# A graph-layer kernel: nineteen whole middle tiles on SyncE's queue in place of fourteen whole and five shared, and no register copy before a row's DMA

## The chip, the cores and the metric

The kernel runs on 1 core of one Trainium2 chip. The metric is the device time of one execution in microseconds. The kernel before takes 1070.66 us, the median of 3 runs (1067.93 to 1071.32). A difference under about 0.3% is no difference that a measurement of this kernel tells.

## What is computed

One relational graph layer with a residual and a normalisation. There are 6250 nodes of 128 features, 106250 edges sorted by destination, and 40 edge types. Cut to what matters:

```
seg = dst * 40 + edge_type
S   = segment_sum(x[src], seg)            # per node and type, 128 features
cnt = segment_sum(1, seg)
agg = einsum('nrd,rdf->nf', S, relation_weights) + cnt @ rFeatures
h   = agg * deg ** -0.5
h   = relu(h + h @ loop_weight)
out = layernorm(x + h)
```

The large irregular part is `x[src]`: 106250 rows of x, fetched by an index that is known only from the input.

## The kernel before

**Tiles and blocks.** The edges are cut into tiles of 128, the nodes into 49 blocks of 128. A block has 17 tiles (`TPB`), 831 tiles are used, and the last of them (tile 830) has 10 edges. For each tile the kernel fetches 128 rows, builds a one-hot matrix of edge types and node positions on VectorE (L815), and multiplies on TensorE (L1027), two matmuls a tile, one for each part of a row: a row of 1 KB in the DRAM tensor `x_parts` holds the features in a high and a low part. ScalarE and VectorE move the result from a PSUM bank into `ring` (L614, L917). Between these, TensorE multiplies the ring by the 40 relation weights and one more matrix (L1039), 82 matmuls (41 pairs) a block. The first 5 blocks fetch plain rows of x instead and split them on the fly, while the same split rows are written to `x_parts` in 13 stages.

**Who fetches the rows.** From block 5 on GpSimd (POOL) fetches a tile with one indirect DMA (L524), in the order of the tiles, into the 17 buffers of `rows`. Before tile t it waits until TensorE is through with tile t - 17 (L523). SyncE (SP) fetches some tiles by itself, row by row: `BY_ROW` lists them, each the middle tile (tile 8 of the 17) of its block, and the last tile. SP's rows go into 8 buffers of their own, which lie in `x_out`, the buffer of the staging; it can begin when the staging is over. For each tile, SP waits until the tile that had its buffer before is done (L471), and then loads up to 16 byte offsets from SBUF into registers (L475), and issues 16 DMAs of one row of 1 KB each, each with a copy of its register (L476, L477). VectorE has made the offsets (L940).

**The shared tiles.** Five of SP's tiles are shared: POOL fetches the first rows of the middle tile in blocks 9, 18, 27, 36 and 45 (126, 124, 127, 112 and 64 of the 128) with one indirect DMA, L509, and SP the rest. SP thus fetches 14 whole tiles (blocks 7, 10, 13 and so on to 46), 87 rows of the shared ones and 10 of the last tile, which is 1889 rows. POOL makes 726 gathers of whole tiles from `x_parts` (L524), 5 of the shared ones, and 85 of plain rows (L531).

**Who waits for the rows.** TensorE waits in `tile` (L1018, L1020) until all rows of the tile have landed. It goes through tiles in order, so a late tile holds all that come after. VectorE waits before its add of tile t (L916) until POOL has issued the gather of tile t + 5.

Of the kernel before, what the change touches and what calls it, by code (L numbers as in the profile page):

```python
# [7 lines left out]
F32 = mybir.dt.float32  # L8
# [3 lines left out]
U8 = mybir.dt.uint8  # L12
F32R = mybir.dt.float32r

P = 128
N, E, D, R = 6250, 106250, 128, 40
# [4 lines left out]
BLOCKS = -(-N // BLOCK)  # L21
LAST_ROWS = N - (BLOCKS - 1) * BLOCK
TPB = 17
# [14 lines left out]
ROW_LOAD = 16  # L38
# [29 lines left out]
FREE_W = 25  # L68
PLAIN_BLOCKS = 5
PLAIN = PLAIN_BLOCKS * TPB  # L70
POOL_PART = {9: 126, 18: 124, 27: 127, 36: 112, 45: 64}
BY_ROW = [i * TPB + TPB // 2 for i in sorted([*range(7, BLOCKS - 1, 3), *POOL_PART])] + [-(-E // P) - 1]
BY_BOTH = {i * TPB + TPB // 2: n for i, n in POOL_PART.items()}
BY_ROW_BUFS = 8
ROW_BYTES = 2 * D * 4
X_ROWS = N // P
# [43 lines left out]
def build(nc, x, src_main, src_by_tile, src_rest, dst_main, dst_rest, type_main, type_rest, r_features, relation_w, loop_w, out):  # L120
    with ExitStack() as ctx:
# [8 lines left out]
        def sem(name):  # L130
            return ctx.enter_context(nc.semaphore(name))
# [141 lines left out]
        by_row_cleared = sem("by_row_cleared")  # L273
        by_row_src_loaded = sem("by_row_src_loaded")
        by_row_ready = sem("by_row_ready")
        both_landed = {t: sem(f"both_landed{t}") for t in BY_BOTH}
        by_row_landed = [sem(f"by_row_landed{j}") for j in range(len(BY_ROW))]
        gathered = [sem(f"gathered{k}") for k in range(TPB)]
        types_ready = sem("types_ready")
# [50 lines left out]
        def rows_in_tile(t):  # L330

            return min(P, E - t * P)

        def first_by_row(t):

            return BY_BOTH.get(t, 0)

        def gathers_through(t):

            return t + 1 - len([n for n in BY_ROW if n <= t and n not in BY_BOTH])  # L340

        def group_of(t):

# [71 lines left out]
        @block.sync  # L415
        def _(sp):
            sp.dma_start(src[:, 0:TPB], src_main[:, 0:TPB]).then_inc(first_src_loaded, 16)
            for t, main in ((dst, dst_main), (typ, type_main)):
                sp.dma_start(t[:, 0:FULL], main).then_inc(edges_loaded, 16)
            sp.wait_ge(padded, 1)  # L420
            for t, rest in ((dst, dst_rest), (typ, type_rest)):
                sp.dma_start(t[0:REST, FULL:FULL + 1], rest).then_inc(edges_loaded, 16)
            sp.dma_start(src[:, TPB:FULL], src_main[:, TPB:FULL]).then_inc(src_loaded, 16)
            sp.dma_start(src[0:REST, FULL:FULL + 1], src_rest).then_inc(src_loaded, 16)

            def stage_load(n):

                p, rows_each, of, _ = stage_rows(n)
                to = x_in[0:p, n % 2, 0:rows_each]
                sp.dma_start(to if rows_each > 1 else to.rearrange("p n d -> p (n d)"), of).then_inc(stage_loaded[n % 2], 16)  # L430

            def stage_store(n):

                p, rows_each, _, to = stage_rows(n)
                of = x_out[0:p, n % 2, 0:rows_each].bitcast(F32)
                sp.wait_ge(stage_low, n + 1)
                sp.dma_start(to, of.rearrange("p n c d -> p n (c d)") if rows_each > 1 else of.rearrange(
                    "p n c d -> p (n c d)")).then_inc(staged[n % 2], 16)

            for n in range(STAGED_FIRST):  # L440
                stage_load(n)
            sp.dma_start(loop[:], loop_w).then_inc(loop_loaded, 16)
            sp.dma_start(x_blk[:], x[0:P, :]).then_inc(x_blk_loaded, 16)
            sp.wait_ge(const_done, 1)
            sp.dma_start(w[0:R, R, :], r_features).then_inc(w_loaded, 16)
            sp.wait_ge(by_row_cleared, 1)
            for j, t in enumerate(BY_ROW):
                of = src_by_tile[t:t + 1, :] if t < FULL else src_rest.rearrange("p o -> o p")
                sp.dma_start(by_row_src[j:j + 1, 0:rows_in_tile(t)], of).then_inc(by_row_src_loaded, 16)
            sp.wait_ge(pos_done, 1)  # L450
            sp.dma_start(pos[:].rearrange("o (b k) -> o b k", k=POS)[:, :, 0:TPB], pos_2d[:, 0:TPB]).then_inc(pos_ready, 16)
            w_v = relation_w.rearrange("r d f -> d r f")
            for r in range(FREE_W, R, W_LOAD):
                sp.dma_start(w[:, r:r + W_LOAD, :], w_v[:, r:r + W_LOAD]).then_inc(w_loaded, 16)
            sp.wait_ge(pos_ready, 16)
            for r in range(0, FREE_W, W_LOAD):
                sp.dma_start(w[:, r:r + W_LOAD, :], w_v[:, r:r + W_LOAD]).then_inc(w_loaded, 16)
            sp.wait_ge(src_loaded, 2 * 16)

            def in_order():  # L460
                for n in range(STAGES):
                    stage_store(n)
                    if n + 2 < STAGES:
                        stage_load(n + 2)
                for h in range(2):
                    sp.wait_ge(staged[h], len(range(h, STAGES, 2)) * 16)
                index = [sp.alloc_register(f"sp_row{n}") for n in range(ROW_LOAD)]
                sp.wait_ge(by_row_ready, 1)
                for j, t in enumerate(BY_ROW):
                    if j >= BY_ROW_BUFS:  # L470
                        sp.wait_ge(tile_done, BY_ROW[j - BY_ROW_BUFS] + 1)  # L471
                    for n, p in enumerate(range(first_by_row(t), rows_in_tile(t))):
                        if n % ROW_LOAD == 0:
                            m = min(ROW_LOAD, rows_in_tile(t) - p)
                            sp.load(index[0:m], by_row_at[j:j + 1, p:p + m])  # L475
                        at = sp.snap(index[n % ROW_LOAD])  # L476
                        sp.dma_start(by_row[p:p + 1, j % BY_ROW_BUFS].rearrange("p c d -> p (c d)").bitcast(U8),  # L477
                                     x_bytes[:, bass.ds(at, ROW_BYTES)]).then_inc(by_row_landed[j], 16)

            def g_load(t):  # L480
                if not isinstance(t, int):
                    sp.wait_ge(g_step, t * G_STEPS + G_SETUP)
                sp.dma_start(g_src[:], src[:, column(t)]).then_inc(g_idx, 16)

            path(sp, in_order, lambda: g_tiles(g_load)(sp))

        @block.gpsimd
        def _(pool):
# [13 lines left out]


            def gather(t):
                if t in BY_BOTH:
                    j, n = BY_ROW.index(t), BY_BOTH[t]
                    if j >= BY_ROW_BUFS:
                        pool.wait_ge(tile_done, BY_ROW[j - BY_ROW_BUFS] + 1)
                    pool.indirect_dma_start(  # L509
                        by_row[0:n, j % BY_ROW_BUFS].rearrange("p c d -> p (c d)").bitcast(F32), None, x_parts,  # L510
                        bass.IndirectOffsetOnAxis(ap=src[0:n, t:t + 1], axis=0), engine_sem=gather_issued).then_inc(
                            both_landed[t], 16)
                    return
                if t in BY_ROW:
                    return
                k = t % TPB
                at_least(pool, gathered[k], gathers_into(k, t - 1) * 16)
                n = rows_in_tile(t)
                if t >= PLAIN:
                    if t == PLAIN:  # L520
                        for h in range(2):
                            pool.wait_ge(staged[h], len(range(h, STAGES, 2)) * 16)
                    pool.wait_ge(tile_done, t - TPB + 1)  # L523
                    pool.indirect_dma_start(  # L524
                        rows[0:n, k].rearrange("p c d -> p (c d)").bitcast(F32), None, x_parts,
                        bass.IndirectOffsetOnAxis(ap=src[0:n, t:t + 1], axis=0), engine_sem=gather_issued).then_inc(
                            gathered[k], 16)
                    return
                if t >= RAW:
                    pool.wait_ge(low_done, group_of(t - RAW) + 1)  # L530
                pool.indirect_dma_start(  # L531
                    raw[:, t % RAW], None, x, bass.IndirectOffsetOnAxis(ap=src[:, t:t + 1], axis=0),
                    engine_sem=gather_issued).then_inc(gathered[k], 16)
# [455 lines left out]
        def _(pe):  # L989
# [12 lines left out]
            def tile(i, k):  # L1002
# [12 lines left out]
                                         hot_node[:, n % TPB], start=True, stop=True)  # L1015
                if not known_less(i, PLAIN_BLOCKS) or not isinstance(i, int):
                    if t in BY_ROW:
                        pe.wait_ge(by_row_landed[BY_ROW.index(t)], (rows_in_tile(t) - first_by_row(t)) * 16)  # L1018
                        if t in BY_BOTH:
                            pe.wait_ge(both_landed[t], 16)  # L1020
                    else:
                        pe.wait_ge(gathered[k], gathers_into(k, t) * 16)
                elif k % 2 == 0:
                    pe.wait_ge(low_done, i * GROUPS + k // 2 + 1)
# [160 lines left out]
```

## Time and profile before

| | |
|---|---|
| median of 3 runs | 1070.66 us |
| the profiled execution | 1068.4 us, its span 1066.5 us |
| TensorE matmul | 954.6 us busy, 90% of the span |
| POOL | 789.6 us busy, 74% |
| VectorE | 742.8 us busy, 70% |
| ScalarE | 532.0 us busy, 50% |
| DMA | 118 GB/s; queue 0 (POOL) 33.5% of the 16 engines, queue 1 (SP) 4.6% |
| mean granted clock of TensorE | 0.985 |

Register moves and the issue of DMAs are not counted as busy, so that SP has no row in this table; its queue (SPq) is read from the timeline and from the rows of its lines. POOL has idle time that is not free: it is the gap from one gather to the next.

### The profile page before, as it was taken

To read this page: it belongs to the slowest core of one execution; us is meant where nothing else is said; L and a number is where in the kernel's file an instruction comes from. 1 tells how busy PE (TensorE), PEld (TensorE's weight loads), DVE (VectorE), ACT (ScalarE), POOL (GpSimd) and SP (SyncE) were. 2 spreads that over 40 slices of the span, in tenths; PEclk is the share of its full clock that TensorE was granted. 3 is DMA by queue.
4 is the path that set the end of the run, shared out by engine and by line. 5 is a ranking of instruction groups with operands and counts; after the bars stand their busy time and mean duration, and the time that the engine had idled before them with its cause. 6 is when DMAs were issued, how large, how long until landed. Compare 5 with 4: busy or idle time off the path is not lost.

```text
span 1066.5 us, 31214 instructions
## 1 busy us (share of the span) xinstructions
PE 954.6 (90%) x6713; PEld 856.4 (80%) x6713; DVE 742.8 (70%) x2590; ACT 532.0 (50%) x1137; POOL 789.6 (74%) x831
## 2 busy tenths in 40 slices
PE   2589999899998989999998899999999899999997
PEld 1369898788888888888887798888888788888887
DVE  6698777676766776667677577767676676767663
ACT  1577555445454545555454355445545554444551
POOL 7777777777777777777777777777777777777770
PEclk9799999999999999999999899999999999999999
DMA  5852234434344443444434344343443344343330
GB/s 166 291 194 56 82 111 116 118 113 115 115 117 113 116 118 112 113 115 118 114 114 115 104 115 114 113 118 112 116 117 114 112 117 118 112 117 112 112 111 23
DMA packets 66376, 125.34 MB, mean 118 GB/s; under 512 B 18074, under 2 KB 37996, under 8 KB 66184
## 3 DMA queue, kind: packets, MB, share of 16 engines
q0 software_dynamic: 38384, 101.36, 33.5%
q1 hardware_dynamic: 13768, 15.61, 4.6%
q10 hardware_dynamic: 14032, 6.35, 2.1%
q8 instruction: 56, 0.92, 0.4%
q14 instruction: 136, 1.11, 0.3%
HBM read 113.63 MB, written 9.60 MB: 116 GB/s over the span
## 4 chain that ended last, share of the span: by engine, by line
PE 42%; DMA 25%; POOL 17%; issue 10%; ACT 1%; DVE 1%; POOLq 0%; SPq 0%; ACTq 0%; DVEq 0%
DMA rows<-x_parts,src 23%; PE win_ps L1027 21%; PE agg_ps L1039 18%; POOL rows L524 16%; PE win_ps L1112 1%; DMA x_in<-x 1%; PE win_ps L1065 1%; POOL raw L531 1%; PE win_ps L1014 1%; DMA x_out<-x_parts,src 0%; ACT ring L614 0%; POOLq L523 0%; PE win_ps L1064 0%; DMA raw<-x,src 0%; DVE ring L917 0%
## 5 line engine op out<-in xcount | busy, mean ns | idle before, releaser
L524 POOL DMA_INDIRECT rows<-x_parts,src x726 | 691.0, 952 | 221.3 <-issue 161.6
L614 ACT COPY ring<-win_ps 128x451 f32 x831 | 465.3, 560 | 371.0 <-PE win_ps L1027 230.7
L1027 PE MATMUL win_ps<-hot,rows 128*128 128x480 f32 x1622 | 557.9, 430 | 62.2 <-DMA rows<-x_parts,src 54.0
L1039 PEld LDWEIGHTS agg_ps<-ring,w 128*128 128x128 f32 x3936 | 554.9, 192 | 41.5
L1039 PE MATMUL agg_ps<-ring,w 128*128 128x128 f32 x3936 | 562.6, 275 | 0.0
L815 DVE TENSOR_SCALAR hot<-iota,key_f 128x480 fp32r<-128x480 f16 x831 | 395.2, 476 | 0.8 <-issue 0.8
L917 DVE TENSOR_TENSOR ring<-ring,win_ps 128x41 f32 x831 | 188.0, 226 | 289.4 <-DMA rows<-x_parts,src 216.7
L1027 PEld LDWEIGHTS win_ps<-hot,rows 128*128 128x128 f32 x1622 | 251.5, 193 | 101.2 <-DMA rows<-x_parts,src 91.1
L531 POOL DMA_INDIRECT raw<-x,src x85 | 90.1, 1060 | 26.0 <-issue 20.1
L1014 PEld LDWEIGHTS win_ps<-hot_node,hot_type 128*128 128x128 bf16 x831 | 80.2, 100 | 34.3 <-issue 16.1
L1014 PE MATMUL win_ps<-hot_node,hot_type 128*128 128x12 bf16 x831 | 85.6, 170 | 22.0 <-DVE ring L917 13.6
L827 DVE TENSOR_TENSOR hot_type<-iota,typ_f 128x320 bf16<-128x320 f16 x98 | 49.8, 508 | 0.0
L646 ACT ACTIVATE var_root<-var_eps 128x1 f32<-128x1 f32 x46 | 9.3, 203 | 58.0 <-DVE var_eps L859 57.9
L638 ACT ACTIVATE deg_root<-deg 128x1 f32<-128x1 f32 x46 | 9.3, 203 | 47.1 <-DVE deg L838 46.8
L875 DVE TENSOR_TENSOR ring<-ring 128x492 f32<-128x492 f32 x48 | 31.9, 665 | 0.0
L887 DVE COPY ring<-zeros 128x492 f32<-128x492 f32 x48 | 31.4, 655 | 0.0
L886 DVE COPY ring<-zeros 128x492 f32<-128x492 f32 x48 | 31.1, 647 | 0.0
L824 DVE TENSOR_TENSOR hot_node<-iota,rel_f 128x96 bf16<-128x96 f16 x98 | 25.1, 256 | 0.4 <-issue 0.4
L1065 PE MATMUL win_ps<-loop,agg_sb 128*128 128x128 f32 x96 | 22.4, 316 | 0.0
L590 ACT CAST rows<-raw 128x256 fp32r<-128x256 f32 (+1 forms) x45 | 17.4, 394 | 8.1 <-DMA raw<-x,src 8.0
L583 ACT CAST x_out<-x_in 128x512 fp32r<-128x512 f32 (+1 forms) x13 | 7.6, 595 | 27.1 <-DMA x_in<-x 13.8
L1027 PE MATMUL win_ps<-hot,x_out 128*128 128x480 f32 x40 | 14.1, 434 | 7.3 <-DMA x_out<-x_parts,src 7.3
(90 smaller groups left out, 281.2 us busy)
## 6 DMA issues: line engine op xcount, KB each, us to landing
x_out<-x_parts SPq DMA_DIRECT2D x1889, 1.0 KB
rows<-x_parts,src POOLq DMA_INDIRECT x726
x_parts<-x_out SPq DMA_DIRECT2D x12, 512.0 KB, 3.2
x_in<-x SPq DMA_DIRECT2D x12, 256.0 KB, 5.2
out<-out_sb ACTq DMA_DIRECT2D x48, 64.0 KB
x_blk<-x ACTq DMA_DIRECT2D x47, 64.0 KB
w<-relation_w SPq DMA_DIRECT2D x8, 320.0 KB
raw<-x,src POOLq DMA_INDIRECT x85
```

Source lines behind the costliest of these rows:

```text
L524: pool.indirect_dma_start(rows[0:n, k].rearrange("p c d -> p (c d)").bitcast(F32), None, x_parts, bass.IndirectOffsetOnAxis(ap=src[0:n, t: ...
L531: pool.indirect_dma_start(raw[:, t % RAW], None, x, bass.IndirectOffsetOnAxis(ap=src[:, t:t + 1], axis=0), engine_sem=gather_issued).then_ ...
L614: nc.scalar.copy(ring[:, :, bass.ds(start + 1, WIN - 1)], win_ps[bank_of(t)][:, :, 1:WIN]).then_inc(copied, 1)
L815: nc.vector.tensor_scalar(hot[:, buffer], iota[:], key_f[:, column(t)], None, ALU.is_equal).then_inc(hot_ready, 1)
L827: nc.vector.tensor_tensor(hot_type[:, at, 0:R], iota[:, 0:R].unsqueeze(1).to_broadcast([P, n, R]), typ_f[:, ts].unsqueeze(2).to_broadcast( ...
L875: nc.vector.tensor_tensor(ring[:, :, bass.ds(head, WIN)], ring[:, :, bass.ds(head, WIN)], ring[:, :, bass.ds(tail + BLOCK, WIN)], ALU.add) ...
L887: nc.vector.tensor_copy(ring[:, :, bass.ds(old + BLOCK, WIN)], zeros[:]).then_inc(cleared, 1)
L917: nc.vector.tensor_tensor(a, a, win_ps[bank_of(t)][:, :, 0:1], ALU.add).then_inc(added, 1)
L1014: nc.tensor.matmul(banks[bank_of(n)][:, R * WIN:COLS * WIN], hot_type[:, n % TPB], hot_node[:, n % TPB], start=True, stop=True)
L1027: ins = nc.tensor.matmul(banks[bank_of(t)][:, 0:R * WIN], of[:, part], hot[:, t % HOTS], start=False, stop=(part == PARTS - 1), skip_group ...
L1039: ins = nc.tensor.matmul(sums_of(c), w[:, r, :], ring[:, r, bass.ds(seg, BLOCK)], start=(r == 0), stop=(r == COLS - 1))
L1065: nc.tensor.matmul(ps[:, 0:D], agg_sb[:], loop[:], start=True, stop=True).then_inc(fin_done, 1)
```

## The change

`BY_ROW` now holds 19 whole middle tiles, in blocks 7, 9, 11, 13, 15, 18, 20, 22, 24, 27, 29, 31, 33, 35, 38, 40, 42, 44 and 47, and the last tile. `POOL_PART`, `BY_BOTH`, L509 and the semaphores of the shared tiles are gone. SP loads each group of 16 offsets into registers that are allocated for it, and the DMA takes the register that was loaded: `snap(reg, donate=True)` makes no copy.

```diff
-POOL_PART = {9: 126, 18: 124, 27: 127, 36: 112, 45: 64}
-BY_ROW = [i * TPB + TPB // 2 for i in sorted([*range(7, BLOCKS - 1, 3), *POOL_PART])] + [-(-E // P) - 1]
-BY_BOTH = {i * TPB + TPB // 2: n for i, n in POOL_PART.items()}
+BY_ROW = [(7 + j * 40 // 18) * TPB + TPB // 2 for j in range(19)] + [-(-E // P) - 1]
...
-                index = [sp.alloc_register(f"sp_row{n}") for n in range(ROW_LOAD)]
                 sp.wait_ge(by_row_ready, 1)
                 for j, t in enumerate(BY_ROW):
                     if j >= BY_ROW_BUFS:
                         sp.wait_ge(tile_done, BY_ROW[j - BY_ROW_BUFS] + 1)
-                    for n, p in enumerate(range(first_by_row(t), rows_in_tile(t))):
-                        if n % ROW_LOAD == 0:
-                            m = min(ROW_LOAD, rows_in_tile(t) - p)
-                            sp.load(index[0:m], by_row_at[j:j + 1, p:p + m])
-                        at = sp.snap(index[n % ROW_LOAD])
-                        sp.dma_start(by_row[p:p + 1, j % BY_ROW_BUFS].rearrange("p c d -> p (c d)").bitcast(U8),
-                                     x_bytes[:, bass.ds(at, ROW_BYTES)]).then_inc(by_row_landed[j], 16)
+                    for first in range(0, rows_in_tile(t), ROW_LOAD):
+                        ps = range(first, min(first + ROW_LOAD, rows_in_tile(t)))
+                        index = [sp.alloc_register(f"sp_row{j}_{p}") for p in ps]
+                        sp.load(index, by_row_at[j:j + 1, ps[0]:ps[-1] + 1])
+                        for p, reg in zip(ps, index):
+                            at = sp.snap(reg, donate=True)
+                            sp.dma_start(by_row[p:p + 1, j % BY_ROW_BUFS].rearrange("p c d -> p (c d)").bitcast(U8),
+                                         x_bytes[:, bass.ds(at, ROW_BYTES)]).then_inc(by_row_landed[j], 16)
+                        for reg in index:
+                            sp.free_register(reg)
...
-                if t in BY_BOTH:
-                    j, n = BY_ROW.index(t), BY_BOTH[t]
-                    if j >= BY_ROW_BUFS:
-                        pool.wait_ge(tile_done, BY_ROW[j - BY_ROW_BUFS] + 1)
-                    pool.indirect_dma_start(
-                        by_row[0:n, j % BY_ROW_BUFS].rearrange("p c d -> p (c d)").bitcast(F32), None, x_parts,
-                        bass.IndirectOffsetOnAxis(ap=src[0:n, t:t + 1], axis=0), engine_sem=gather_issued).then_inc(
-                            both_landed[t], 16)
-                    return
```

On POOL's queue, from block 5 to the end, there stands before:

```order
L524 DMA rows<-x_parts,src 128x256 x75
L509 DMA x_out<-x_parts,src 126x256
L524 DMA rows<-x_parts,src 128x256 x149
L509 DMA x_out<-x_parts,src 124x256
L524 DMA rows<-x_parts,src 128x256 x149
L509 DMA x_out<-x_parts,src 127x256
L524 DMA rows<-x_parts,src 128x256 x149
L509 DMA x_out<-x_parts,src 112x256
L524 DMA rows<-x_parts,src 128x256 x149
L509 DMA x_out<-x_parts,src 64x256
L524 DMA rows<-x_parts,src 128x256 x55
```

and now

```order
L517 DMA raw<-x,src 128x128 x68
L510 DMA rows<-x_parts,src 128x256 x726
L379 UNCONDITIONAL_BRANCH
```

The gathers of whole tiles are as many as before, 726, and the five of the shared tiles between them are gone.

On SP's queue, in the second of its tiles (block 9), there stands before the end of the tile of block 7, then 2 rows of the shared tile, then the tile of block 10:

```order
L475 TENSOR_LOAD by_row_at
L477 DMA x_out<-x_parts 1x1024 x16
L475 TENSOR_LOAD by_row_at
L477 DMA x_out<-x_parts 1x1024 x2
L475 TENSOR_LOAD by_row_at
L477 DMA x_out<-x_parts 1x1024 x16
```

and now, in the same place, the whole tile of block 9:

```order
L467 TENSOR_LOAD by_row_at
L470 DMA x_out<-x_parts 1x1024 x16
L467 TENSOR_LOAD by_row_at
L470 DMA x_out<-x_parts 1x1024 x16
L467 TENSOR_LOAD by_row_at
L470 DMA x_out<-x_parts 1x1024 x16
```

SP has 153 loads and 2442 row DMAs where it had 121 and 1889; the copies of registers (L476), which these rows leave out, go from 1889 to none.

On TensorE, in the middle of block 47, the last full block, there stands before

```order
L1014 MATMUL win_ps<-hot_node,hot_type 128x12 x2
L1027 MATMUL win_ps<-hot,rows 128x480 x2
L1039 MATMUL agg_ps<-ring,w 128x128 x3
L1027 MATMUL win_ps<-hot,rows 128x480 x2
```

and now, where `x_out` holds SP's rows and `rows` POOL's,

```order
L1000 MATMUL win_ps<-hot_node,hot_type 128x12 x2
L1011 MATMUL win_ps<-hot,x_out 128x480 x2
L1023 MATMUL agg_ps<-ring,w 128x128 x3
L1011 MATMUL win_ps<-hot,rows 128x480 x2
```

The number and the order of TensorE's matmuls stay; the middle tile of block 47 now comes from SP, whose last whole tile was that of block 46.

## Rows read from the trace of the kernel before

**Rows 1.** Page: busy time by engine, then the chain that ended last.

```profile
span 1066.5 us, 31214 instructions
PE 954.6 (90%) x6713; PEld 856.4 (80%) x6713; DVE 742.8 (70%) x2590; ACT 532.0 (50%) x1137; POOL 789.6 (74%) x831
PE 42%; DMA 25%; POOL 17%; issue 10%; ACT 1%; DVE 1%; POOLq 0%; SPq 0%; ACTq 0%; DVEq 0%
```

**Rows 2.** Waits: engine and line, who ended them, us in total, times, longest us.

```profile
POOL rows L524 <- issue: 161.6, 530, 0.3
POOL rows L524 <- PE win_ps L1027: 59.8, 196, 0.3
PEld win_ps L1027 <- DMA rows<-x_parts,src: 91.1, 169, 2.0
PE win_ps L1027 <- DMA rows<-x_parts,src: 54.0, 93, 1.8
```

**Rows 3.** Windows: us, then PE, PEld, DVE, ACT, POOL busy (instructions), clock, DMA, GB/s.

```profile
595.00:600.00 5.00, 1.12 (x10) 0.95 (x9) 3.21 (x12) 1.27 (x3) 3.78 (x5) 1.00 0.45 128
600.00:605.00 5.00, 3.68 (x14) 3.43 (x15) 0.00 (x0) 0.34 (x1) 3.78 (x5) 0.54 0.40 118
605.00:610.00 5.00, 5.00 (x33) 4.59 (x32) 2.40 (x11) 2.40 (x7) 4.04 (x4) 0.78 0.40 122
610.00:650.00 40.00, 40.00 (x304) 37.58 (x303) 31.80 (x116) 23.39 (x50) 30.46 (x31) 1.00 0.39 112
700.00:800.00 100.00, 92.58 (x656) 83.13 (x655) 69.69 (x246) 49.67 (x105) 75.68 (x80) 1.00 0.41 115
```

**Rows 4.** SP's lines L475 to L477: duration in ns (min/median/max), first and last start.

```profile
L475 SPq TENSOR_LOAD <-by_row_at x121: 556/1250/1418, 75.6 to 973.0; - x121
L476 SPq MOVE  x1889: 34/34/48, 76.8 to 978.1; - x189
L477 SPq MOVE x_out<-x_parts x1889: 29/29/39, 76.8 to 978.2; - x189
L477 SPq DMA_DIRECT2D x_out<-x_parts x1889: 224/225/732, 76.9 to 978.2; - x189
```

**Rows 5.** Timeline of SP: start us, length us, queue, line, operation.

```profile
6.34 5.26 SPq L449 DMA_DIRECT2D by_row_src<-src_by_tile  x18
...
11.94 0.25 SPq L449 DMA_DIRECT2D by_row_src<-src_rest  x1
...
76.93 901.54 SPq L477 DMA_DIRECT2D x_out<-x_parts  x1889
```

**Rows 6.** Timeline of SP, inside one group of 16 rows.

```profile
299.79 4.11 SPq L477 DMA_DIRECT2D x_out<-x_parts  x11
```

**Rows 7.** Timeline of PE: middle tiles of blocks 7, 46, 47; tile 830; last matmul.

```profile
176.78 0.68 PE L1027 MATMUL win_ps<-hot,x_out 128*128 128x480 f32 x2
...
993.15 0.68 PE L1027 MATMUL win_ps<-hot,x_out 128*128 128x480 f32 x2
...
1015.65 0.70 PE L1027 MATMUL win_ps<-hot,rows 128*128 128x480 f32 x2 [0.76 <-DMA rows<-x_parts,src]
...
1042.54 0.69 PE L1027 MATMUL win_ps<-hot,x_out 128*128 128x480 f32 x2
...
1060.48 0.47 PE L1116 MATMUL win_ps<-loop,agg_sb 128*106 128x128 f32 x2 [0.34 <-ACT agg_sb L714]
```

**Rows 8.** DMA issues: line, count, KB each, median us from issue to landing.

```profile
x_parts<-x_out SPq DMA_DIRECT2D x12, 512.0 KB, 3.2
src<-src_main SPq DMA_DIRECT2D x1, 8.5 KB, 1.8
```

**Rows 9.** Windows of L614 alone, one copy a tile: us, busy (copies), clock, DMA, GB/s.

```profile
610.00:650.00 40.00, 21.39 (x39) 1.00 0.39 112
700.00:800.00 100.00, 45.40 (x81) 1.00 0.41 115
```

**Rows 10.** Timeline of PE at the shared tile of block 27.

```profile
601.32 1.14 PE L1027 MATMUL win_ps<-hot,x_out 128*128 128x480 f32 x2 [5.21 <-DMA x_out<-x_parts,src]
```

More of the change, by code:

```diff
@@ L275, in build @@
         by_row_ready = sem("by_row_ready")
-        both_landed = {t: sem(f"both_landed{t}") for t in BY_BOTH}
         by_row_landed = [sem(f"by_row_landed{j}") for j in range(len(BY_ROW))]
@@ L332, in rows_in_tile @@
             return min(P, E - t * P)
-        def first_by_row(t):
-            return BY_BOTH.get(t, 0)
         def gathers_through(t):
-            return t + 1 - len([n for n in BY_ROW if n <= t and n not in BY_BOTH])
+            return t + 1 - len([n for n in BY_ROW if n <= t])
         def group_of(t):
@@ L1017, in tile @@
                     if t in BY_ROW:
-                        pe.wait_ge(by_row_landed[BY_ROW.index(t)], (rows_in_tile(t) - first_by_row(t)) * 16)
-                        if t in BY_BOTH:
-                            pe.wait_ge(both_landed[t], 16)
+                        pe.wait_ge(by_row_landed[BY_ROW.index(t)], rows_in_tile(t) * 16)
                     else:
```

## The prediction

> **What bounds the kernel now.** I read the page first, then the waits, the windows, and last SP's queue. The page [rows 1] shows TensorE at 90% and POOL at 74%, and a chain shared among PE, DMA, POOL and "issue". The reader should not stop at 90%. In the windows POOL starts 80 gathers in each 100 us [rows 3], one per 1.25 us, and no gap before a gather is over 0.3 us [rows 2]: POOL never stops, its gaps are its own pace. TensorE in turn waits for POOL's rows, 54.0 us, and its weight loads 91.1 us, in short pieces of 2.0 us at most [rows 2]. So POOL sets the pace, and TensorE has little room under it. How much shows after a stall: from 610 to 650 us TensorE is busy all 40.00 us [rows 3] with its rows already there, and finishes about 38 to 39 tiles, 1.04 us a tile, where the steady pace is 81 in 100 us, 1.23 us [rows 9].
>
> SP is in no table of busy time, but its queue is as full as POOL's. Its 1889 rows run from 76.93 us for 901.54 us [rows 5]. Take away 120 loads between them at 1.25 us [rows 4], and a row costs (901.54 - 150.0) / 1888 = 0.398 us. A group of 16 rows costs 16 x 0.398 + 1.25 = 7.62 us, a whole tile 61 us. SP is ahead of TensorE, not by much: the tile of block 46 is issued by 973.0 us, where the load of the last tile starts [rows 4], and used at 993.15 us [rows 7]. So the margin at the end is 20 us.
>
> **POOL's side of the change.** Five gathers fewer at 1.25 us: 6.25 us off the pace that sets the end. A wait goes too: TensorE stood 5.21 us for the shared tile of block 27 [rows 10], and its clock fell from 1.00 to 0.54 and 0.78 in the next two windows [rows 3], near the lower of its two levels (1.2 of 2.4 GHz). I credit nothing for that: POOL went on through it, 5 gathers in each 5 us, and TensorE caught up by itself. On that side the gain is 6.25 us, if the rows that SP now fetches come in time.
>
> **SP's side: the price of a row.** Removed: one MOVE a row (34 ns). The MOVE at L477 (29 ns) and the DMA (225 ns) stay. These three make 288 ns. Inside a group the pitch is (4.11 - 0.225) / 10 = 388 ns [rows 6], so 100 ns lie between the three instructions, 33 each. The MOVE is worth at least its own 34 ns and at most, with its share of the gaps, 67 ns. The other bound is a row DMA with no MOVE at all beside it: L449, 18 of them in 5.26 us with 0.25 us each, a pitch of (5.26 - 0.25) / 17 = 295 ns [rows 5]; the gap behind each is 42 ns there, which says that every instruction of SP carries a gap. So the MOVE's price is nearer to 67 than to 34; I take 60. The new row costs 0.398 - 0.060 = 0.338 us, with bounds of 0.305 (0.295 and the 0.010 by which the average, 0.398, lies above the pitch of 0.388) and 0.364 (0.398 less the bare 34 ns).
>
> By the Trainium skill (Perfetto Trace Analysis, Per-engine timelines) the profile reports only the execution of a sequencer's instruction, and fetch, decode and the push of its semaphore lie outside. It speaks for more than 34 ns; the gaps of [rows 6] agree.
>
> **SP's side: the sum.** A group: 16 x 0.338 + 1.26 = 6.67 us. A tile: 8 groups, 53.3 us. There are 19 instead of some 14.7, so SP needs 19 x 53.3 = 1013 us for the whole tiles alone. It starts at 75.6 us as before [rows 4], since the staging isn't touched. Tile number j (from 0) is issued at 75.6 + 53.3 (j + 1): the last, that of block 47, at 1089 us. Landing adds 2 us (bounds 1.8 and 3.2, the two landings that the table of issues has for SP [rows 8]): 1091.
>
> TensorE wants that tile at 1015.65 us at today's pace [rows 7], less 6.25, so at 1009.4. It comes 82 us too late. The lateness builds up evenly. TensorE goes 2.2 blocks from one of SP's tiles to the next, 38 tiles at 1.25 us less one, some 46 us, and SP takes 53.3. SP starts with a lead of about 45 us (first tile at 129, wanted at 176.78 [rows 7]) and loses it at 7 to 8 us a tile, so that from the seventh or eighth tile, near 500 us, TensorE stands at every tile of SP, and SP sets the pace. POOL then waits for TensorE (L523), 17 tiles ahead, which costs nothing more. SP's own waits for a buffer (L471) are far: tile j needs what was in tile j - 8, over 200 us earlier.
>
> **The end.** Before, 50.85 us lay between the first matmul of block 47's middle tile and the end (1066.5 - 1015.65). Of these, 26.9 us are the 23 tiles to tile 830 (1042.54 - 1015.65 [rows 7]). Now POOL's rows for them lie ready, so they go at 1.04 us, 24.0 us, 2.9 less. A stall of this size costs clock: after the stall of block 27 the windows lost 5 x 0.46 + 5 x 0.22 = 3.4 us of full-speed time [rows 3]. The two cancel: plus 0.5. Tile 830's 10 rows come 5 us after, in time. The span is 1091 + 50.9 + 0.5 = 1142.5 us. With the 1.9 us that the profiled execution had over its span (1068.4 against 1066.5) it is **1144 us**. That execution lies 2.3 us under the median of the runs, which is small here.
>
> One check: the way from block 44 to block 47 is three blocks, 51 tiles at 1.04 us and 3.4 us of lost clock, 56.4 us, where SP gives 53.3. TensorE then reaches the tile 3 us after it is there, and no clock is lost behind it: the same end, within a microsecond.
>
> **The rivals.**
> *The rows come in time.* Then the five gathers count and the time is 1068.4 - 6.25 = 1062 us, **faster**. It has one threshold. The last tile must be issued by 1009.4 - 2 = 1007 us, so a tile in 49.0 us, a group in 6.13, a row in 0.304. The MOVE would have to give back 94 ns, nearly all the gaps of a row [rows 6]. For it speaks the 295 ns of L449 alone, which sits just at that point; against it, that L449 has no register in its address and no MOVE before it. A few nanoseconds around the threshold decide, so a time within 0.3% of the old one lies in this rival's margin (0.304 to 0.308). The Trainium skill (DMA: Bandwidth & Descriptors, Issuing engines are not separate DMA queues) says that issuing from more engines saves only the sequencer's time to initiate, "which is usually small relative to the DMA itself"; by that SP would be no bound, and this rival is what would follow. In this trace the initiation is the whole cost: SP's queue moves 4.6% of the DMA engines' time and is never free. I give it 0.10, and 0.03 to the margin.
>
> *The MOVE is worth its 34 ns only.* Row 0.364, tile 56.7, last tile issued at 1153, end near 1206 + 1.9 = 1208 us. The gaps speak against it: 0.04.
>
> *The change doesn't do what it says.* If the pace of SP were set by what takes the DMAs behind it and not by its instructions, the MOVE would be hidden and a row would stay at 0.398: tile 61.0, last tile at 1235, time near 1290 us. Against it: the DMA's duration stays at 224 to 225 ns from minimum to median, no sign of a queue that pushes back. 0.03.
>
> *The MOVE is worth 67 ns.* Row 0.331, tile 52.4, end 17 us earlier: 1127 us. This is inside my case, as is a row of 0.345 with 1160 us.
>
> **How the numbers follow.** My case (SP late, row between 0.321 and 0.348) has 0.80, the slower rivals 0.07, the faster one 0.10, the margin 0.03. Faster by over 0.3% (about what a measurement here tells): 0.10; same 0.03; slower 0.87. The likeliest time is 1144 us; ten nanoseconds of a row are 2432 x 0.010 = 24 us, so the range is 1104 to 1168 us, and the 0.20 outside it are the other cases.
>
> **What would show it.** SP's timeline: 2442 rows with no MOVE of its own line, pitch 0.33 us within a group, the last whole tile issued near 1089 us and the last row near 1093. The waits: a large total for win_ps at TensorE behind the DMA of x_out, stalls of up to 10 us, some eleven of them, from about 500 us on. The windows: before 450 us all as now; after, clock under 1.00 in every other window, POOL under 80 gathers in 100 us (near 70). I am wrong if the pitch is under 0.30 us, if the wait behind x_out is a few us in total, or if POOL still has 80 gathers in each 100 us at the end.

## The result, and the profile after

The changed kernel takes 1127.65 us, the median of 6 runs (1126.82 to 1135.39), where the kernel before took 1070.76 us beside it (6 runs, 1067.93 to 1071.49): a ratio of 1.055, 95% interval 1.052 to 1.059. It is slower by 57 us. The six times lie in two groups, 1126.8 to 1128.0 and 1134.5 to 1135.4, and the profiled execution is of the lower one. The forecast was 1144 us in a range of 1104 to 1168.

The page of the changed kernel: the span, the busy times, then the chain by engine and by line.

```profile
span 1124.9 us, 30453 instructions
PE 944.2 (84%) x6713; PEld 865.4 (77%) x6713; DVE 736.1 (65%) x2590; ACT 531.9 (47%) x1137; POOL 800.7 (71%) x826
SPq 65%; issue 15%; PE 14%; DMA 1%; DVE 1%; ACT 0%; DVEq 0%; ACTq 0%; POOLq 0%
SPq L470 50%; SPq L467 15%; PE agg_ps L1023 7%; PE win_ps L1011 5%; PE win_ps L1096 1%; DMA x_in<-x 0%; DMA x_parts<-x_out 0%; DMA x_out<-x_parts 0%; PE win_ps L1049 0%; PE win_ps L1000 0%; DVE x_out L790 0%; PE win_ps L1048 0%; ACT ring L600 0%; DVE hot L801 0%; DMA raw<-x,src 0%
```

Against [rows 1], every engine does about the same work in a longer span, and the chain, which had 0% of SP's queue, now has 65% of it: L470, the row DMAs, and L467, the loads of the offsets.

The waits of the changed kernel (engine and line, who ended them, total us, times, longest us):

```profile
POOL rows L510 <- issue: 182.8, 597, 0.7
PEld win_ps L1011 <- DMA x_out<-x_parts: 109.4, 9, 14.3
PE win_ps L1011 <- DMA x_out<-x_parts: 108.5, 9, 14.2
POOL rows L510 <- PE win_ps L1011: 84.9, 129, 10.0
```

TensorE stood nine times for one of SP's tiles, 108.5 us in all. The time grew by 57 us, so about half of that was won back elsewhere, in the main between the stalls. POOL, whose gaps had all been 0.3 us at most [rows 2], now waits up to 10.0 us for TensorE: it ran its 17 tiles ahead and stopped.

SP's two lines in the changed kernel (duration in ns min/median/max, first and last start), and its timeline:

```profile
L467 SPq TENSOR_LOAD <-by_row_at x153: 1148/1252/1466, 73.6 to 1069.1; - x153
L470 SPq MOVE x_out<-x_parts x2442: 29/29/42, 74.8 to 1073.3; - x188
L470 SPq DMA_DIRECT2D x_out<-x_parts x2442: 224/225/316, 74.9 to 1073.3; - x188
```

```profile
74.90 998.67 SPq L470 DMA_DIRECT2D x_out<-x_parts  x2442
```

The durations are those of [rows 4], and the 34 ns copy is gone. A row costs (998.67 - 0.22 - 152 x 1.252) / 2441 = 0.331 us where it cost 0.398: the copy was worth 67 ns. A tile takes 8 x (16 x 0.331 + 1.252) = 52.4 us. The load for tile 830 starts at 1069.1, so that the last whole tile is issued by then; this is how the issue of SP's last whole tile is read in all runs below.

TensorE's timeline in the changed kernel, at the tiles of SP in blocks 24, 44 and 47:

```profile
545.50 1.17 PE L1011 MATMUL win_ps<-hot,x_out 128*128 128x480 f32 x2 [13.99 <-DMA x_out<-x_parts]
...
1017.89 1.17 PE L1011 MATMUL win_ps<-hot,x_out 128*128 128x480 f32 x2 [13.15 <-DMA x_out<-x_parts]
...
1074.62 0.68 PE L1011 MATMUL win_ps<-hot,x_out 128*128 128x480 f32 x2
```

Two rows of the windows of the changed kernel (columns as in [rows 3]):

```profile
560.00:600.00 40.00, 40.00 (x303) 37.62 (x303) 30.91 (x112) 22.88 (x49) 30.85 (x31) 1.00 0.39 110
700.00:800.00 100.00, 77.96 (x548) 72.84 (x548) 57.60 (x204) 41.93 (x88) 64.18 (x66) 0.88 0.34 95
```

The stretch from 700 to 800 us had 80 gathers and a clock of 1.00 [rows 3]; it has 66 and 0.88 now. The clock is low behind the stalls: the two matmuls at 1017.89 take 1.17 us, those at 1074.62, where nothing was waited for, 0.68.

### The profile page after: what moved, and what is told of

It is laid out like the page before. It is cut to its first block, busy times and chain, and to the rows that moved or that the text cites. A ratio compares the mean times of both kernels' runs of the same rounds, so it can differ in the third digit from the quotient of the medians.

```text
span 1124.9 us, 30453 instructions
## 1 busy us (share of the span) xinstructions
PE 944.2 (84%) x6713; PEld 865.4 (77%) x6713; DVE 736.1 (65%) x2590; ACT 531.9 (47%) x1137; POOL 800.7 (71%) x826
## 4 chain that ended last, share of the span: by engine, by line
SPq 65%; issue 15%; PE 14%; DMA 1%; DVE 1%; ACT 0%; DVEq 0%; ACTq 0%; POOLq 0%
SPq L470 50%; SPq L467 15%; PE agg_ps L1023 7%; PE win_ps L1011 5%; PE win_ps L1096 1%; DMA x_in<-x 0%; DMA x_parts<-x_out 0%; DMA x_out<-x_parts 0%; PE win_ps L1049 0%; PE win_ps L1000 0%; DVE x_out L790 0%; PE win_ps L1048 0%; ACT ring L600 0%; DVE hot L801 0%; DMA raw<-x,src 0%
## 5 line engine op out<-in xcount | busy, mean ns | idle before, releaser
L510 POOL DMA_INDIRECT rows<-x_parts,src x726 | 710.0, 978 | 267.7 <-issue 182.8
L1023 PEld LDWEIGHTS agg_ps<-ring,w 128*128 128x128 f32 x3936 | 566.0, 195 | 42.9
L1023 PE MATMUL agg_ps<-ring,w 128*128 128x128 f32 x3936 | 572.5, 279 | 0.0
L1011 PEld LDWEIGHTS win_ps<-hot,rows 128*128 128x128 f32 x1622 | 256.2, 196 | 47.4 <-DMA rows<-x_parts,src 38.5
L1011 PE MATMUL win_ps<-hot,x_out 128*128 128x480 f32 x40 | 18.0, 540 | 108.5 <-DMA x_out<-x_parts 108.5
L1000 PEld LDWEIGHTS win_ps<-hot_node,hot_type 128*128 128x128 bf16 x831 | 81.5, 100 | 33.7 <-issue 15.5
L1011 PEld LDWEIGHTS win_ps<-hot,x_out 128*128 128x128 f32 x40 | 7.8, 244 | 109.4 <-DMA x_out<-x_parts 109.4
L1048 PEld LDWEIGHTS win_ps<-ones,cnt_sb 128*128 128x128 f32 x96 | 18.2, 191 | 3.3 <-ACT agg_sb L619 0.5
```

The costliest lines, as they stand in the source:

```text
L510: pool.indirect_dma_start(rows[0:n, k].rearrange("p c d -> p (c d)").bitcast(F32), None, x_parts, bass.IndirectOffsetOnAxis(ap=src[0:n, t: ...
L1000: nc.tensor.matmul(banks[bank_of(n)][:, R * WIN:COLS * WIN], hot_type[:, n % TPB], hot_node[:, n % TPB], start=True, stop=True)
L1011: ins = nc.tensor.matmul(banks[bank_of(t)][:, 0:R * WIN], of[:, part], hot[:, t % HOTS], start=False, stop=(part == PARTS - 1), skip_group ...
L1023: ins = nc.tensor.matmul(sums_of(c), w[:, r, :], ring[:, r, bass.ds(seg, BLOCK)], start=(r == 0), stop=(r == COLS - 1))
```

## The experiments

Each ratio is to the kernel before, on the same chip. The kernels leave nothing out of the computation.

**1. The direct register alone, with the old tiles.** Edit to the kernel before, cut to the line that counts (the registers are allocated afresh for each group of offsets, as in the changed kernel):

```diff
-                        at = sp.snap(index[n % ROW_LOAD])
+                            at = sp.snap(reg, donate=True)
```

> Edit to the kernel before: SP's register copy is taken out (the DMA takes the loaded register), the tiles and the shared five stay. Theory (POOL's 1.25 us a gather sets the pace, SP only has to be in time): SP's row falls from 0.398 to 0.33 us, SP ends near 845 instead of 978 us, and the time stays at 1070.7 us within 0.3%. Rival (SP's queue is part of the bound of the kernel before, so that a shorter row is time won): the time falls, by up to 1889 x 0.068 = 128 us if SP were all of the bound, by over 0.3% if a part.

Measured: ratio 1.000 (0.999 to 1.001). The timeline of SP in this run:

```profile
76.17 775.04 SPq L477 DMA_DIRECT2D x_out<-x_parts  x1889
```

SP is through at 851 us, 127 us earlier than in [rows 5], and nothing is won. The shorter row is no gain where SP is in time; what the change does to the time comes through the tiles it hands from POOL to SP.

**2. The copy put back, with the new tiles.** Edit to the changed kernel:

```diff
-                            at = sp.snap(reg, donate=True)
+                            at = sp.snap(reg)
```

> Edit to the changed kernel: the register copy before each row's DMA is put back, all else stays. Theory (SP's queue sets the end, and the copy is worth its 34 ns and about as much of gap): a row takes 0.398 us instead of 0.329, a tile 61 us, the last whole tile is issued near 1235 us, the time is 1285 to 1295 us, 165 us more. Rival (the gain of the shorter row came from the fresh registers and the grouping of the loads, not from the missing copy): the row stays at 0.33 and the time near 1128 us.

Measured: 1291.3 us (2 runs), ratio 1.207 (1.204 to 1.210). SP's timeline, and the line of the copy (duration in ns, first and last start):

```profile
75.63 1162.56 SPq L470 DMA_DIRECT2D x_out<-x_parts  x2442
```

```profile
L469 SPq MOVE  x2442: 34/34/48, 75.5 to 1237.8; - x188
```

SP's rows take 1162.56 instead of 998.67 us: 163.9 us for 2442 copies, 67 ns each. The time goes up by 163.7 us beside the changed kernel's; its two runs lie 6.6 us apart, and between the two profiled executions the span grows by 161.3 us (1124.9 to 1286.2). So SP's queue sets the end there, nearly one for one, the rival falls, and an instruction of 34 ns costs twice its duration.

**3. Loads of 32.** Edit to the changed kernel:

```diff
-ROW_LOAD = 16
+ROW_LOAD = 32
```

> Edit to the changed kernel: SP loads 32 offsets at a time, not 16. In the trace of before a load of 2 takes 0.556 and one of 16 takes 1.250 us, 50 ns a register and 0.45 us fixed. Theory (every 1 us of SP's tile counts 19 times): a load of 32 takes 2.05 us, a tile 50.3 instead of 52.4 us, the last whole tile comes 39 us earlier, and the time is near 1088 us. Rival (a load costs by the register alone, 2.5 us for 32): 1127 us. Rival (TensorE, with its clock, sets the end and not SP): less than 20 us gained.

Measured: 1097.0 us (4 runs), ratio 1.025 (1.023 to 1.026). The load's line in this run:

```profile
L467 SPq TENSOR_LOAD <-by_row_at x77: 1291/2164/2362, 75.1 to 1038.5; - x77
```

A load of 32 takes 2.16 us, not 2.05, and a tile 50.7 us. The last whole tile is issued 30.6 us earlier (1038.5 against 1069.1), and the median falls by 30.6 us too, the span of the profiled execution by 28.3 (1124.9 to 1096.6). The theory's cause holds, with the load's price 0.1 us too low, so that 1097 and not 1088 us came out; the two rivals fall.

**4. The last tile one block earlier.** Edit to the changed kernel:

```diff
-BY_ROW = [(7 + j * 40 // 18) * TPB + TPB // 2 for j in range(19)] + [-(-E // P) - 1]
+BY_ROW = [(7 + j * 40 // 18 - j // 18) * TPB + TPB // 2 for j in range(19)] + [-(-E // P) - 1]
```

> Edit to the changed kernel: SP's 19th whole tile is that of block 46 instead of 47. SP issues it at the same time, 1069 us. Theory (in the changed kernel TensorE went the three blocks from 44 to 47 at its own pace and came to the tile some 4 us after it had landed): now it stands at block 46 for about 14 us and has one block more to do behind it, 13 to 17 us more, 1141 to 1145 us. Rival (the end hangs on SP's last tile alone, and 47 was waited for as well): 18 to 20 us more. Rival (the sum of TensorE's work sets the end): 1128 us.

Measured: 1147.35 us (4 runs, 1143.09 to 1152.07), its span 1141.3 us, 16.4 us over that of the changed kernel. TensorE at block 46's tile:

```profile
1070.05 1.17 PE L1011 MATMUL win_ps<-hot,x_out 128*128 128x480 f32 x2 [14.11 <-DMA x_out<-x_parts]
```

The stall is the 14 us that were expected. The median lies just above the expected stretch, and 19.7 us above the changed kernel's, which would be the first rival's figure. But its four times lie in two pairs, at 1143 and at 1151 to 1152, as the changed kernel's do at 1127 to 1128 and at 1135. Like with like, the step is 16 to 17 us, and 16.4 us by the spans, inside the theory's 13 to 17. The stall says the same: in the changed kernel the tile of block 47 was not waited for. The rival of 1128 us falls.

**5. Eighteen tiles, each where SP is in time.** Edit to the changed kernel:

```diff
-BY_ROW = [(7 + j * 40 // 18) * TPB + TPB // 2 for j in range(19)] + [-(-E // P) - 1]
+BY_ROW = [(5 + (5 * j + 1) // 2) * TPB + TPB // 2 for j in range(18)] + [-(-E // P) - 1]
```

> Edit to the changed kernel: 18 whole middle tiles in place of 19, each in a block that TensorE reaches after SP has it: blocks 5, 8, 10, 13, 15, 18 and so on to 45 and 48; the direct register stays. SP's tile takes 52.3 us, so tile j is there at 73.6 + 52.3 (j + 1) + 2 us: 128 us for block 5 (reached at 137 us), 1017 for block 48 (reached near 1031). Theory (the changed kernel loses only by lateness, and POOL's gathers set the pace otherwise): no stall behind x_out over 1 us, POOL makes 727 gathers from x_parts where the kernel before made 731, 4 x 1.25 = 5 us less, time near 1065.7 us, ratio 0.995 to before. Rival (whole tiles of SP, or 2314 rows of it, cost something of their own, by contention or by clock): the time stays over 1070 us although SP is in time.

Measured: 1061.3 us (7 runs), ratio 0.9951 (0.9933 to 0.9970). It is faster than both kernels. Its waits:

```profile
PE win_ps L1011 <- DMA x_out<-x_parts: 3.9, 3, 2.8
```

```profile
700.00:800.00 100.00, 92.29 (x657) 83.50 (x656) 70.14 (x246) 49.85 (x105) 75.61 (x81) 1.00 0.41 116
```

SP fetches 2314 rows here without great harm, and POOL is back at 80 to 81 gathers in 100 us. One stall of 2.8 us, at block 45, is more than was expected. POOL's gathers in this run (count, busy us, mean ns):

```profile
L510 POOL DMA_INDIRECT rows<-x_parts,src x727 | 691.0, 951 | 221.7 <-issue 161.6 <-PE win_ps L1011 60.0
```

The 5.2 us that are won are what 4 gathers fewer at 1.25 us give, but that agreement is partly luck. The shared gather of 127 rows, worth 3.7 us by run 9, is gone here too. Beside run 9, which was measured on the same chip, this run wins only 2.4 us (1063.8 to 1061.3), not 5. In the profiled executions POOL's last gather starts 4.1 us earlier (1029.4 against 1033.6), and 29.0 us lie behind it where there were 28.0.

**6. Nineteen tiles, as far as possible in time.** Edit to the changed kernel, beside loads of 32:

```diff
-BY_ROW = [(7 + j * 40 // 18) * TPB + TPB // 2 for j in range(19)] + [-(-E // P) - 1]
+BY_ROW = [b * TPB + TPB // 2 for b in [5, 8, 10, 12, 15, 17, 20, 22, 25, 27, 29, 32, 34, 37, 39, 42, 44, 46]] + [LAST * TPB + 12, USED - 1]
```

> Edit to the changed kernel: 19 whole tiles and the last one as there, but SP loads 32 offsets at a time, and the tiles stand where TensorE comes after them: middle tiles of blocks 5, 8, 10, 12, 15, 17 and so on to 46, and tile 828, the 13th of block 48. Theory (lateness alone made the changed kernel slower): no stall over 3 us, POOL makes 726 gathers, time 1059 to 1062 us, ratio 0.992 to 0.995 to before. Rival (19 whole tiles from SP cost something that 18 did not): over 1065 us.

Measured: 1069.2 us (12 runs), ratio 1.0005 (0.998 to 1.003). That is over the stretch of the theory and, by its number, where the rival had it. TensorE at tiles 828 and 830:

```profile
1038.61 1.04 PE L1011 MATMUL win_ps<-hot,x_out 128*128 128x480 f32 x2 [1.87 <-DMA x_out<-x_parts]
...
1043.08 0.70 PE L1011 MATMUL win_ps<-hot,x_out 128*128 128x480 f32 x2 [0.39 <-DMA x_out<-x_parts]
```

It was not in time at the end: SP has issued tile 828 only at 1037.6 us (loads of 32 take 2.16 us here too, not the 2.05 of the plan), and TensorE waited for both of the last tiles, in a stretch where nothing is left to hide it. Run 3 has the same loads and the same number of tiles and differs in their places alone: it took 1097.0 us, so of what the changed kernel lost the places give back 27.8 us, and the longer loads had given back 30.6. By the ratios this run is 5.8 us behind run 5 (the two were measured on different chips, so the plain times do not compare). Most of that lies at the end: 33.7 us from the start of POOL's last gather to the end of the span, where run 5 has 29.0. What is left, 1.1 us and the gather that is spared, bounds what the 19th tile itself can cost at some 2 us; no run with 19 tiles was fully in time.

**7. Eighteen tiles, spread evenly.** Edit to the changed kernel:

```diff
-BY_ROW = [(7 + j * 40 // 18) * TPB + TPB // 2 for j in range(19)] + [-(-E // P) - 1]
+BY_ROW = [(7 + j * 40 // 17) * TPB + TPB // 2 for j in range(18)] + [-(-E // P) - 1]
```

> Edit to the changed kernel: 18 whole middle tiles in place of 19, spread evenly over the same blocks, 7 to 47; direct register, loads of 16. SP issues the last one near 1016 us, and TensorE, which in the run with 18 tiles in time came to the middle of block 47 at 1008 us, wants it 8 to 10 us sooner than it lands. Theory (only the lateness at the end is paid, nearly one for one, less 2 to 3 us that TensorE regains on the rows that lie ready): 5 to 8 us more than that run, ratio to before 0.999 to 1.003, one or a few stalls behind x_out. Rival (the number of tiles decides and not where they stand): the same as that run, ratio 0.995.

Measured: 1081.8 us (4 runs), ratio 1.0135 (1.011 to 1.016): slower than the theory's 1.003 at most. The expectation looked only at the last tile. In fact TensorE stood 11.4 us at the tile of block 44, which it reached far ahead of SP, and then took 56.5 us over the three blocks to 47 (966.7 to 1023.2), at its own pace and without a wait, where SP had been sooner.

**8. The last two tiles one block later.** Edit to run 7's kernel:

```diff
-BY_ROW = [(7 + j * 40 // 17) * TPB + TPB // 2 for j in range(18)] + [-(-E // P) - 1]
+BY_ROW = [(7 + j * 40 // 17 + (j > 15)) * TPB + TPB // 2 for j in range(18)] + [-(-E // P) - 1]
```

> Edit to the run with 18 even tiles (1081.8 us, span 1073.4): the last two of SP's whole tiles stand one block later, 45 and 48 in place of 44 and 47; the other 16 and all of SP's work stay. There TensorE stood 11.4 us at block 44's tile, which SP had issued at 965 us, and needed 55 us for the three blocks behind it, while SP's own last tile was there before. Theory (a late tile holds TensorE once, and the blocks behind it go at TensorE's pace, 18.3 us each, so that the end is the latest of SP's arrivals plus the blocks that are left behind it): from 967 us at block 45 to 1022 us at block 48, one block more done by the same time, about 15 us less, 1062 to 1068 us. Rival (the stalls at the tiles before, blocks 32, 37 and 39, are paid each for itself): 1075 us or more, 6 us or less gained.

Measured: ratio 1.0028 (1.001 to 1.0045), 1073.2 us (12 runs). The theory was half right: 1.07 points of ratio are won, 11 us, more than the rival gave, and no stall is left behind block 39. But 15 us and 1062 to 1068 were missed. The waits, POOL's gathers, and its timeline at the last stall:

```profile
PE win_ps L1011 <- DMA x_out<-x_parts: 26.5, 3, 14.4
```

```profile
L510 POOL DMA_INDIRECT rows<-x_parts,src x727 | 700.0, 963 | 224.6 <-issue 168.5 <-PE win_ps L1011 56.2
```

```profile
864.84 0.95 POOL L510 DMA_INDIRECT rows<-x_parts,src  x1 [2.29 <-PE win_ps L1011]
...
868.07 0.95 POOL L510 DMA_INDIRECT rows<-x_parts,src  x1 [1.03 <-PE win_ps L1011]
```

A stall of 14.4 us is long enough for POOL to come 17 tiles ahead and stop, and POOL is the resource that sets the pace: those 2.7 us (2.29 and 1.03 less two gaps of 0.30) are not won back. More is lost in the gathers themselves, for the reason that run 11 shows: the same 727 gathers take 700.0 us here and 691.0 in run 5. Together that is 11.7 of the 12.3 us between the two profiled spans (1070.7 and 1058.4). By the ratios, which leave the difference of the chips out, run 8 is 8.2 us behind run 5. So a late tile in the middle does cost something, though far less than its stall.

**9. The shared tile of block 27.** Edit to the kernel before:

```diff
-POOL_PART = {9: 126, 18: 124, 27: 127, 36: 112, 45: 64}
+POOL_PART = {9: 126, 18: 124, 27: 112, 36: 112, 45: 64}
```

> Edit to the kernel before: in block 27 POOL fetches 112 rows of the shared tile, not 127, and SP 16. Theory (the 5.2 us for which TensorE stood at that tile costs nothing, since POOL went on at its pace): the stall at about 601 us is gone or under 1 us, the clock stays at 1.00 there, and the time stays at 1070.7 us within 0.3%. Rival (the stall and the low clock behind it are paid): 5 to 9 us less, ratio 0.992 to 0.995.

Measured: 1063.8 us (6 runs), ratio 0.9965 (0.9953 to 0.9977), 3.7 us less. The stall is gone. The expectation of no change was wrong, by little; the rival's size was not reached either. POOL's gathers in this run, whole and shared (count, busy us, mean ns):

```profile
L524 POOL DMA_INDIRECT rows<-x_parts,src x726 | 688.7, 949 | 221.3 <-issue 158.8 <-PE win_ps L1027 62.5
...
L509 POOL DMA_INDIRECT x_out<-x_parts,src x5 | 5.0, 1008 | 1.5 <-issue 1.5
```

The same two groups in the kernel before, and its L509 by single gathers:

```profile
L524 POOL DMA_INDIRECT rows<-x_parts,src x726 | 691.0, 952 | 221.3 <-issue 161.6 <-PE win_ps L1027 59.8
...
L509 POOL DMA_INDIRECT x_out<-x_parts,src x5 | 6.7, 1333 | 1.5 <-issue 1.2 <-PE win_ps L1027 0.3
```

```profile
L509 POOL DMA_INDIRECT x_out<-x_parts,src x5: 907/987/2548, 214.9 to 969.3; - x5
...
DMA to landing us min/median/max: 2.6/3.9/10.3
```

The gather of 127 rows held POOL for 2.55 us and took 10.3 us to land. On POOL, 1.7 us come back from the shared gathers and 2.3 us from the whole ones, 4.0 us where 3.7 were measured: the gain is time of POOL. The stall has a share in it. Of the 2.3 us, 1.4 lie in the 45 gathers of the 60 us behind it, which take 977 ns on average in the kernel before and 946 here; TensorE catches up there, and run 11 shows what that does to gathers. How large that share is stays uncertain: runs 1 and 10, on the same chip as run 9, keep the stall, and their whole gathers take 692.5 and 689.9 us. The Trainium skill (DMA: Bandwidth & Descriptors, Why a DMA increments its semaphore by 16 and not by 1) says that a transfer is shared among the largest number of DMA engines, up to 16, that divides its partitions, so that 127 partitions go to one. By that 112 would go to 16 and 124 to 4. The trace agrees in direction: 10.3 us to landing with 127 rows, 5.0 with 124, at most 4.8 in run 9.

**10. One wait in place of two on POOL.** Edit to the kernel before:

```diff
-                at_least(pool, gathered[k], gathers_into(k, t - 1) * 16)
+                if t < PLAIN:
+                    at_least(pool, gathered[k], gathers_into(k, t - 1) * 16)
```

> Edit to the kernel before: from block 5 on POOL does not wait for the landing of the gather that filled its buffer last, only for TensorE to be through with that tile, which comes later; each gather thus has one wait in place of two instructions with a wait. Theory A (the 0.30 us between two gathers is time of POOL's queue, of which the second wait is a part): a gather takes 1.25 us less 0.06 or more, 731 x 0.06 = 44 us less, down to where TensorE's 1.04 us a tile takes over, near 900 us in all. Theory B (the gap belongs to the gather itself): 1.25 us as before and the time within 0.3%.

Measured: ratio 0.999 (0.998 to 1.000). POOL's timeline in this run:

```profile
700.93 0.94 POOL L525 DMA_INDIRECT rows<-x_parts,src  x1 [0.30 <-issue]
702.17 0.95 POOL L525 DMA_INDIRECT rows<-x_parts,src  x1 [0.30 <-issue]
```

The 0.30 us stay to the hundredth. Theory A falls: the second wait is no part of the gap, and 1.25 us is what a gather costs with one wait or two. What fills the 0.30 us no run here shows.

**11. VectorE without its wait for POOL's issue.** Behind the stall of block 27 in the kernel before, gathers had taken up to 1.17 us. POOL's timeline there:

```profile
606.35 1.10 POOL L524 DMA_INDIRECT rows<-x_parts,src  x1 [0.30 <-issue]
...
610.26 1.17 POOL L524 DMA_INDIRECT rows<-x_parts,src  x1 [0.30 <-issue]
```

Edit to the kernel before:

```diff
-BEHIND = 5
+BEHIND = 0
```

> Edit to the kernel before: VectorE's add of tile t waits until POOL has issued the gather of tile t itself (always long past), not of tile t + 5, so that VectorE no longer starts behind an issue of POOL. In the traces gathers take 1.02 to 1.17 us, and not 0.95, where TensorE catches up after a stall and VectorE works without that wait. Theory (VectorE's work and a gather get in each other's way, and the wait keeps them apart): the mean gather rises from 0.952 us by 0.01 to 0.03, and 731 of them cost 7 to 20 us more, ratio 1.006 to 1.02. Rival (the longer gathers come from the DMA engines or from the higher rate of all engines, not from VectorE's starts): mean and time as before, within 0.3%.

Measured: 1102.6 us (5 runs), ratio 1.031 (1.030 to 1.033), more than the theory's 1.02. POOL's whole gathers in this run (count, busy us, mean ns), then a piece of POOL's timeline and of VectorE's:

```profile
L524 POOL DMA_INDIRECT rows<-x_parts,src x726 | 723.4, 996 | 221.4 <-issue 174.4 <-PE win_ps L1027 47.0
```

```profile
701.92 0.95 POOL L524 DMA_INDIRECT rows<-x_parts,src  x1 [0.30 <-issue]
703.17 1.15 POOL L524 DMA_INDIRECT rows<-x_parts,src  x1 [0.31 <-issue]
704.63 1.09 POOL L524 DMA_INDIRECT rows<-x_parts,src  x1 [0.30 <-issue]
```

```profile
702.90 0.23 DVE L917 TENSOR_TENSOR ring<-ring,win_ps 128x41 f32 x1
703.04 0.46 DVE L815 TENSOR_SCALAR hot<-iota,key_f 128x480 fp32r<-128x480 f16 x1
```

The same 726 gathers hold POOL for 32.4 us more than in the kernel before (723.4 against 691.0), and the time is about 33 us longer. The gather of 703.17 started while VectorE was at its one-hot, from 703.04 on, and took 1.15 us. Counted over the whole trace: 252 of the 726 gathers start while a one-hot of L815 runs and take 1066 ns on average, the other 474 take 959. In the kernel before only 21 gathers start so, and take 1094 ns against 948. The 252 gathers hold 30 us more than 0.947 us each would, which is nearly all of the 32.4. With the wait of L916, VectorE starts behind an issue of POOL, and the two mostly keep apart.

## Why the prediction was right, and where it was off

**What bounds before: right.** POOL's pace at 1.25 us a gather set the time. Run 1 took 127 us from SP and changed nothing; run 11 put 32.4 us on POOL's gathers and cost 33. In the kernel before and in runs 1, 9, 10 and 11 the span ends 28.0 to 28.4 us after POOL's last gather starts, though the spans go from 1061.6 to 1100.8 us. Run 5 is the weaker witness, as said there.

**SP late, and the side of the result: right.** Nineteen tiles took SP past TensorE from about 493 us on (forecast: near 500), the chain is SP's queue, and runs 2 and 3 move the time by what they add to it or take from it, within 3 us.

**The price of a row: mis-sized.** The step "I take 60", for a MOVE between 34 and 67 ns, should have taken the upper bound. The copy is worth 67 ns: by subtraction (0.398 to 0.331) and by run 2. With 0.331 the prediction's own sum gives the 1127 us that it names among its cases. The 17 us between 1144 and 1127 are 2432 rows at 7 ns. The gap of 33 ns behind each instruction was read from [rows 6], and there was no reason to shade it. That the sum with 0.331 meets the measured time to a microsecond is partly luck: SP began 2 us earlier (73.6, not 75.6), its loads took 1.2 us less in all and the last stretch 1.1 us less, while TensorE came 3.5 us after the landing, where the main sum had it waiting there.

**The end: right on the way to block 47, two errors against each other behind it.** From block 44's tile to block 47's TensorE took 56.7 us (forecast 56.4) and came 3.5 us after the landing (forecast 3), if 2 us of landing hold. That is the case of the prediction's check, and there the rest should have taken 48.0 us (50.9 less the 2.9 of ready rows, with no clock lost). It took 50.3, because the last 23 tiles went in 26.4 us (1074.6 to 1101.0), not in 24.0: TensorE was busy throughout at a granted clock of 1.00, so the pace of 1.04 us a tile, read from 610 to 650 us, does not hold in the last blocks. The 50.9 + 0.5 of the main sum came close only because they held a loss of clock that did not happen. The last whole tile was issued at 1069 instead of 1089 us, which is in the main the price of the row again.

**What the profile would show: mostly right.** Forecast were eleven stalls of up to 10 us; there were 9, of up to 14.2. POOL made 66 gathers in 100 us instead of 70.

**"I credit nothing for that": wrong, by up to 4 us.** The five shared gathers were taken at 1.25 us each, but one took 2.55 us, and gathers behind its stall took longer (run 9). "5 gathers in each 5 us" misread the third window of [rows 3]: from 605 to 610 us it has 4 gathers and 4.04 us of busy time, where run 9 has 5 and 3.78. It is small beside 57 us and hidden by them.

## What to carry to other kernels

A queue that only issues has a capacity like an engine, though no table of busy time has it: count its instructions from start to start, with the gaps, not by their durations, and compare the sum with the time by which the last consumer needs it. When a stream of late-bound pieces is shared between a fast and a slow supplier, place the slow one's pieces by its own arrival times and not evenly: here 18 tiles in time were 0.5% faster than the kernel before and 18 even ones 1.35% slower. A stall is won back only as fast as the consumer outruns the pace, and only while the pacing engine isn't stopped by it.

## What the runs showed that was not expected

**POOL's gather depends on when VectorE works.** Its mean duration is 0.952 us where VectorE starts behind POOL's issue and 0.996 us where it doesn't (run 11), with 0.30 us of gap in both. The changed kernel has this effect too: POOL is many tiles ahead while TensorE catches up, the wait of L902 holds nothing back then, and the mean gather is 0.978 us where it was 0.952.

```profile
L510 POOL DMA_INDIRECT rows<-x_parts,src x726 | 710.0, 978 | 267.7 <-issue 182.8 <-PE win_ps L1011 84.9
```

In the changed kernel SP hides it; in run 8 POOL sets the pace again behind the stalls, and pays. The Trainium skill (SBUF — State Buffer, Who interferes with whom) says that GpSimd and VectorE share a pair of ports as an exclusive lock, which an operation like `tensor_scalar` can take in its two-port modes. The trace agrees: L815 is a `tensor_scalar`, and the long gathers are in the main those that start while it runs, 1066 against 959 ns (run 11), in the changed kernel 1054 against 952. That it is the ports and nothing else the two share is not shown by a run.

**A register copy of 34 ns costs 67 ns** on SP's queue, measured twice: by taking it out (0.398 to 0.331 us a row) and by putting it back (163.9 us for 2442).

**A gather of 127 rows** held POOL 2.55 us and landed 10.3 us after its issue, where, with 112 in its place (run 9), none of the five took over 1.29 us:

```profile
L509 POOL DMA_INDIRECT x_out<-x_parts,src x5: 907/929/1292, 213.4 to 964.6; - x5
```

**A wait less on POOL changes nothing:** 0.30 us lie between two gathers with two waits or with one (run 10).

What stays open: what fills the 0.30 us between two gathers, how much of run 9's 3.7 us is the slow gather itself and how much the stall behind it, and whether 19 tiles that are all in time would reach run 5.
